# The two halves of each accumulator, added by a DMA with addition on GpSimd's queue in place of VectorE's addition

## What is computed

```
hidden = x
for i in (0, 1, 2):
    z   = einsum('bmd,bnd->bmnd', x, hidden).reshape(B, -1, D)
    cur = relu(einsum('bcd,co->bod', z, W[i]) + b[i])
    layers 0, 1: hidden, direct = cur[:, :100], cur[:, 100:]
    layer 2:     direct = cur
out = concatenate(direct of all layers).sum(-1)
```

## Time and profile before

| | before |
|---|---|
| median of 3 runs | 2800.74 us (2798.97 to 2800.89) |
| profiled execution, its own time | 2799.83 us |
| its span in the trace | 2798.1 us |
| granted clock of PE, mean | 0.997 of full speed |
| PE busy | 2707.5 us (97%) |
| DVE busy | 2722.4 us (97%) |
| ACT busy | 1763.7 us (63%) |
| POOL busy | 1.2 us, 11 instructions |

### The profile page before, as it was taken

How to read it: one execution, slowest core, us unless ns; L and a number is a source line. 1 busy time by engine, 2 the same in 40 slices (tenths; PEclk the granted TensorE clock), 3 DMA queues, 4 the chain that set the end, 5 groups by cost and what they waited for, 6 DMA issues and landing times.

```text
span 2798.1 us, 56046 instructions
## 1 busy us (share of the span) xinstructions
PE 2707.5 (97%) x18112; PEld 2642.5 (94%) x18112; DVE 2722.4 (97%) x3090; ACT 1763.7 (63%) x3178; POOL 1.2 (0%) x11
## 2 busy tenths in 40 slices
PE   1799999999999999999999999999999999999998
PEld 1799999999999999999999999999999999999998
DVE  3899999999999999999999999999999999999997
ACT  2566666666666666666666666666666666666664
POOL 0000000000000000000000000000000000000000
PEclk9999999999999999999999999999999999999999
DMA  8454544454454454454454454454454445444441
GB/s 193 110 126 109 129 123 108 118 134 108 123 129 109 112 138 110 117 131 112 109 138 114 113 130 117 108 132 120 108 128 121 111 122 129 109 117 124 119 112 54
DMA packets 346786, 333.97 MB, mean 119 GB/s; under 512 B 151970, under 2 KB 281614, under 8 KB 346638
## 3 DMA queue, kind: packets, MB, share of 16 engines
q1 hardware_dynamic: 346762, 333.67, 47.7%
HBM read 332.73 MB, written 8.37 MB: 122 GB/s over the span
## 4 chain that ended last, share of the span: by engine, by line
PE 93%; DMA 3%; DVE 1%; ACT 1%; SPq 1%; issue 1%; ACTq 0%; DVEq 0%
PE acc L620 63%; PE acc L621 28%; DMA xb<-x_by_unit 1%; PE summed L638 1%; PE turned L632 1%; DMA xb<-in_L_rec_b_dram 1%; ACT z_high L495 0%; DMA w_rows_again<-in_L_rec_W_dram 0%; DVE z_low L354 0%; DMA xb<-in_L_rec_W_dram 0%; DVE w_split L327 0%; ACT w_split L523 0%; ACT hid L514 0%; DVE z L350 0%; SPq L170 0%
## 5 line engine op out<-in xcount | busy, mean ns | idle before, releaser
L620 PE MATMUL acc<-w_split,z_high 128*128 128x400 f32 (+1 forms) x8832 | 2656.2, 368 | 71.8 <-DVE z_low L354 64.7
L621 PE MATMUL acc<-w_split,z_low 128*128 128x200 f32 (+1 forms) x8832 | 2252.9, 255 | 0.0
L620 PEld LDWEIGHTS acc<-w_split,z_high 128*128 128x128 f32 (+1 forms) x8832 | 1662.2, 188 | 119.8 <-issue 86.2
L495 ACT ACTIVATE z_high<-z 128x1024 fp32r<-128x1024 f32 (+2 forms) x1152 | 1181.9, 1026 | 898.1 <-DVE z L350 812.6
L621 PEld LDWEIGHTS acc<-w_split,z_low 128*128 128x128 f32 (+1 forms) x8832 | 1691.4, 192 | 0.0
L354 DVE TENSOR_TENSOR z_low<-z,z_high 128x1024 fp32r<-128x1024 f32 (+2 forms) x1152 | 1373.2, 1192 | 7.7 <-ACT z_high L495 7.0
L350 DVE TENSOR_TENSOR z<-hid,xb 128x1024 f32<-128x1024 f32 (+1 forms) x1024 | 1232.2, 1203 | 8.4 <-ACT hid L514 5.4
L514 ACT ACTIVATE hid<-turned 32x128 f32<-32x128 f32 x768 | 205.3, 267 | 8.9
L511 ACT ACTIVATE hid<-turned 96x512 f32<-96x512 f32 x256 | 150.1, 586 | 35.1 <-PE turned L632 33.3
L361 DVE TENSOR_TENSOR s<-acc,half 128x200 f32<-128x200 f32 x384 | 144.6, 377 | 9.8 <-ACT half L500 9.8
L339 DVE TENSOR_TENSOR z<-x_left,x_right 118x896 f32<-118x896 f32 x128 | 140.2, 1096 | 0.0
(11 more groups left out here) (21 smaller groups left out, 35.9 us busy)
## 6 DMA issues: line engine op xcount, KB each, us to landing
xb<-x_by_unit SPq DMA_DIRECT2D x384, 384.0 KB, 4.3
x_right<-x_by_unit SPq DMA_DIRECT2D x384, 136.5 KB
xb<-x_by_unit SPq DMA_DIRECT2D x384, 128.0 KB, 4.9
xb<-x_by_unit SPq DMA_DIRECT2D x128, 336.0 KB
xb<-x_by_unit SPq DMA_DIRECT2D x128, 84.0 KB
x_left<-x_by_unit SPq DMA_DIRECT2D x384, 19.5 KB
xb<-in_L_rec_W_dram SPq DMA_DIRECT2D x6, 600.0 KB, 8.6
x_by_unit<-in_r_x_dram SPq DMA_DIRECT2D x128, 19.5 KB
```

What stands on the lines that cost most here:

```text
L495: nc.scalar.activation(z_high[slot][0:rows, 0:n * T], z[slot][0:rows, 0:n * T], ACT.Copy).then_inc(high, 1)
L620: nc.tensor.matmul(a[:, 0:2 * O], z_high[slot][0:rows, tok], w, start=(c == 0), stop=False, skip_group_check=True)
L621: last = nc.tensor.matmul(a[:, 0:O], z_low[slot][0:rows, tok], w[:, 0:O], start=False, stop=(c == chunks - 1), skip_group_check=True)
```

## The change

The addition leaves DVE. ACT copies both halves of `acc[l]` to SBUF in one instruction (400 columns in place of 200), the first half to where `s[l]` lies and the second beside it, in one tensor `both[l]`. GpSimd then issues a DMA that adds the second to the first in place (`fold`), and its landing raises `s_in[l]` by 16. PE may write the accumulator anew as soon as ACT's copy is done.

```diff
-        s = {0: sb("s0", [P, 2, P]), 1: sb("s1", [P, 2, P]), 2: sb("s2", [P, 2, HID])}
-        half = {l: sb(f"half{l}", [P, 2, HID]) for l in range(3)}
+        both = {0: sb("both0", [P, 2, 2, P]), 1: sb("both1", [P, 2, 2, P]), 2: sb("both2", [P, 2, 2, HID])}
+        s = {l: both[l][:, 0, :, :] for l in range(3)}
...
+            def fold(l, u):
+                pool.wait_ge(half_in[l], u + 1)
+                pool.dma_start(s[l][:, :, 0:HID], both[l][:, 1, :, 0:HID], accum_op=ALU.add).then_inc(s_in[l], 16)
+
+            def period(n, layer0=True):
+                fold(1, n)
+                if layer0:
+                    fold(0, n + 2)
+                fold(2, n - 1)
...
-            def sums(l, u):
-                dve.wait_ge(half_in[l], u + 1)
-                if not (isinstance(u, int) and u == 0):
-                    dve.wait_ge(direct_in[l], u)
-                nc.vector.tensor_tensor(s[l][:, :, 0:HID], acc[l][:, 0:O].rearrange("p (h o) -> p h o", o=HID), half[l][:, :, :], ALU.add)\
-                  .then_inc(s_in[l], 1)
-
             def directs(l, rows, q):
...
-                dve.wait_ge(s_in[l], u + 1)
+                dve.wait_ge(s_in[l], 16 * (u + 1))
...
-                sums(1, n)
...
-                if layer0:
-                    sums(0, n + 2)
...
-            def second_half(l, u, last):
+            def halves(l, u, last):
 
                 act.wait_ge(freed, RING + last + 1)
-                nc.scalar.activation(half[l][:, :, :], acc[l][:, O:2 * O].rearrange("p (h o) -> p h o", o=HID), ACT.Copy)\
+                if not (isinstance(u, int) and u == 0):
+                    act.wait_ge(direct_in[l], u)
+                nc.scalar.activation(both[l][:, :, :, 0:HID], acc[l][:, 0:2 * O].rearrange("p (k h o) -> p k h o", k=2, o=HID), ACT.Copy)\
                   .then_inc(half_in[l], 1)
 
             def dup(l, u):
-                act.wait_ge(s_in[l], u + 1)
+                act.wait_ge(s_in[l], 16 * (u + 1))
...
             def acc_free(l, u):
-                pe.wait_ge(s_in[l], u)
+                pe.wait_ge(half_in[l], u)
```

More of the change, by code:

```diff
@@ L317, in _ @@
                                     base=STEPS - 1, pattern=[[STEPS, BT]], channel_multiplier=-1).then_inc(consts, 1)
+            def fold(l, u):
[6 more added lines that the diff above has]
+                fold(2, n - 1)
+            fold(0, 0)
+            fold(0, 1)
+            fold(1, 0)
+            fold(0, 2)
+            for n in range(1, UNITS):
+                period(n, layer0=n + 2 < UNITS)
+            fold(2, UNITS - 1)
         @block.vector
@@ L400, in _ @@
                     lows(1, 1, L0_ROWS, L0_CHUNKS)
-                    sums(0, 0)
                 if k == 2:
                     directs(0, 0, 0)
-                if k == 3:
-                    sums(0, 1)
             dve.wait_ge(w_low_done, 1 + 2 * GROUPS)
@@ L418, in _ @@
             lows(at + 4, slot_of(at + 4), L0_ROWS, L0_CHUNKS)
-            sums(1, 0)
-            sums(0, 2)
             directs(1, 0, 0)
@@ L441, in period @@
                 lows(base + 2, slot(2), P, group_chunks(2))
-                if before2:
-                    sums(2, n - 2)
                 q = 4
@@ L479, in _ @@
             product12(2, UNITS - 1, 1, 0, at, slot_of(at))
-            sums(2, UNITS - 2)
             for g in range(1, GROUPS):
@@ L485, in _ @@
             lows(at + 3, slot_of(at + 3), P, group_chunks(3))
-            sums(2, UNITS - 1)
             directs(2, last, 3)
@@ L533, in _ @@
                     highs(1, 1, L0_ROWS, L0_CHUNKS)
-                    second_half(0, 0, 0)
+                    halves(0, 0, 0)
                     act.wait_ge(consts, 4)
@@ L538, in _ @@
                     hidden(0, 0, 0)
-                    second_half(0, 1, 1)
+                    halves(0, 1, 1)
                 if k == 5:
@@ L548, in _ @@
             highs(at + GROUPS, slot_of(at + GROUPS), L0_ROWS, L0_CHUNKS)
-            second_half(1, 0, at + 3)
-            second_half(0, 2, at + 4)
+            halves(1, 0, at + 3)
+            halves(0, 2, at + 4)
             dup(1, 0)
@@ L566, in period @@
                 if before2:
-                    second_half(2, n - 2, base - 1)
+                    halves(2, n - 2, base - 1)
                 if j == 0:
@@ L580, in period @@
                 highs(base + q + 1, slot(q + 1), P, group_chunks(1))
-                second_half(1, n, base + 3)
+                halves(1, n, base + 3)
                 highs(base + q + 2, slot(q + 2), P, group_chunks(2))
                 if layer0:
-                    second_half(0, n + 2, base + 4)
+                    halves(0, n + 2, base + 4)
                 if before2 and j == 1:
@@ L601, in _ @@
             hidden(1, UNITS - 1, 1)
-            second_half(2, UNITS - 2, at - 1)
+            halves(2, UNITS - 2, at - 1)
             for g in range(GROUPS):
@@ L605, in _ @@
             results(1, last)
-            second_half(2, UNITS - 1, at + 3)
+            halves(2, UNITS - 1, at + 3)
             results(2, last)
```

## The result

| | before | changed |
|---|---|---|
| median | 2800.81 us (2798.97 to 2801.43, 4 runs) | 3326.22 us (3309.96 to 3335.73, 4 runs) |
| ratio | | 1.187, 95% interval 1.182 to 1.192 |
| span of the profiled execution | 2798.1 us | 3322.3 us |
| mean granted clock of PE | 0.997 | 0.942 |

The changed kernel is slower by 525 us, or 18.7%. The prediction had the sign and the place of the loss, but 52 us in place of 525, and the time lies far above its range.

A forecast was written before the change was run, and what follows sets the result against it. DVE was taken as the bound by a hair over PE. A middle period of 20.23 + 4.9 - 3.75 = 21.38 us adds 39 us over 125 periods, the ends 13 us: 2852 us, 1.8% slower, range 2768 to 2990 us.

The forecast's parts named there:

- What bounds the kernel: In the long middle DVE fills its 21.07 us period without slack; PE follows at about 20.76 us.
- The price of the additions: Three additions per period leave DVE, 0.28 us each, 0.84 us together, so DVE's work falls to 20.23 us.
- ACT's wider copy: ACT's copy of 400 columns takes 0.51 us, adding 0.5 us per period, hidden as ACT is 63% busy.
- The window of 3.75 us: DVE waits at `directs(1)` only if L, from ACT's copy end to the landing DVE sees, is over 3.75 us.
- The formula 20.23 + (L - 3.75): DVE's period in us: its work without additions plus what L, copy's end to landing, exceeds the window by.
- L = 4.9 us: Time from the end of ACT's copy to the landing DVE sees, taken from a 128 KB `xb` load's landing.
- The upper bound of 6.8 us: Bound from above on L, copy's end to landing: the longest landing of an `xb` load.
- I cost that at nothing too: The added DMA bytes, about 0.3 MB per period beside 2 MB of `xb` loads, were claimed to cost nothing.
- Rival 1: The sum lands inside its window, L under 4.3 us, and PE is the bound: 2779 us, 0.8% faster; chance 0.37.
- the draw: L between 4.3 and 4.6 us: the wait at `directs(1)` eats the additions' gain; 2794 to 2806 us; chance 0.07.
- Rival 3: Making GpSimd's DMA pieces waits for DVE instructions, L grows up to 1.13 us to 6.0 us: 2996 us; chance 0.08.
- `dup` on ACT: `dup(1)` stood 4.0 us after the copy's end; it follows DVE's wait for the sum and does not lead it.

The follow-up runs named there:

- The best kernel: Changed kernel with later readers of layer 1 and 0 sums and layer 0's store issued after the token loads: 2773.6 us, ratio 0.991.
- experiment 4: Changed kernel with the readers of the sums of layers 1 and 0 put two to three groups later: 2801.3 us, ratio 1.0008.
- experiment 2: Changed kernel with each xb load from unit 2 on bringing one chunk in place of up to eight: 2798.9 us.
- experiment 1: Changed kernel with GpSimd's DMAs copying the second half over the first instead of adding it: 3019.5 us.
- experiment 6: Changed kernel with layers 1 and 0 laid out as 128 pieces of 800 bytes per DMA in place of 256 of 400: 3250.7 us.
- experiment 5: Changed kernel with layer 0's store issued after the token loads: 3246.9 us; also with late readers: 2773.6 us; both moves with additions on DVE: 2794.8 us.
- experiment 9: Changed kernel with 24 small matmuls on PE ahead of layer 2's last group; sums not right, only time read: 3276.5 us.
- experiment 3: Changed kernel with only layer 2's sum by DMA, layers 1 and 0 added by DVE as before: 2785.8 us, ratio 0.9956.
- experiment 7: Changed kernel with plain copies in place of the additions, issued from ACT's queue instead of GpSimd's: 3228.6 us.
- experiment 8: Changed kernel with only layer 1's sum by DMA, the other two added on DVE: 3376.4 us.

## Why the prediction was wrong

**What bounds the kernel: right.** DVE full at 21.07 us, PE close behind at 20.76 us. The best kernel, in which PE alone is the bound, ran at 20.82 us per period.

**The price of the additions, 0.84 us for three: right.** In experiment 4, in the three periods of four in which DVE stood for at most 0.05 us, its period was 20.28 us, where the prediction had 20.23 us. What the time could gain was less, as foreseen, because PE follows: 0.16 us a period for layer 2 alone, 0.25 us for all three with late readers and the moved store.

**ACT's wider copy, 0.51 us and hidden: right** (0.51 us at 1508.86, and 0.498 us on average for L502).

**The window of 3.75 us: right.** The formula 20.23 + (L - 3.75) gives 23.4 us for the L of 6.9 measured above, and 44 periods at full clock lasted 23.9 us on average. Experiment 4 removed the loss by moving the readers alone, with landings as long as before.

**L = 4.9 us: this is the step that failed.** The term "I take 4.9 us, the landing of the 128 KB load" was measured as 6.9 us in the period shown and 10.1 us in a fourth one (copy's end at 1556.31, sum at 1566.37); over the periods from 300 to 2600 us the median was 7.3 us, and 9.2 us in the fourth ones. Two things were taken wrongly. The landing of an `xb` load counts from its issue, while L also has the 0.3 us from ACT to GpSimd. And the adding DMA is another kind of transfer: with thin loads its L is already 3.9 us (experiment 2), and beside the loads it is held up more than an `xb` load is, 7.0 us from issue to landing against 5.0 us for the 128 KB load in the same kernel. Why it is held up more stays open in part. A plain copy in few packets landed in 5.0 us (experiment 1), but making the pieces twice as large changed layer 1's landing by only 0.2 us (experiment 6), so their size of 400 bytes is not the reason. Two windows of the DMA list show the hold-up, from the issue at 1509.66 to about the first of its packets, and from there to the landing:

```profile
q1 hardware_dynamic: 201, 0.68, 101.3%
```

```profile
q1 hardware_dynamic: 368, 0.67, 72.3%
q0 software_dynamic: 458, 0.17, 41.0%
```

From 1509.6 to 1512.4 us only the loads' queue has packets, at 101% of all engines. The sum's queue has its first one at 1512.68, 3.0 us after the issue, where it took 1.8 us with thin loads, and needs until 1516.2. (The 458 packets of the second window are those of layer 1's sum and of a part of layer 0's.) I had seen the engines' share of 1.00, called it a reason for a larger value, and then let a favourable reason cancel it. The upper bound of 6.8 us was no bound: it was a landing of another kind of transfer, and L reached 11.3 us.

The Trainium skill's price (DMA: Bandwidth & Descriptors, Anatomy of one DMA — SWDGE (gpsimd) path), about 2.0 us fixed plus bytes at 436 GB/s, an estimate of 2.2 us here, comes near where nothing else runs: 2.5 to 2.8 us from issue to landing for layer 2's adding DMA, 1.9 us for the shortest plain copy. Beside the loads the measurement was 6.6 us for the DMA shown, 4.4 us more than the estimate.

**"I cost that at nothing too" for the traffic beside the loads: wrong in size as well.** The cover over the `xb` loads held, and no wait on `xb` became long. But a fourth period that was a little late before was made worse by the long waits (the store ahead of the loads: 79 us by experiment 5), and PE ran at half clock after many of its pauses (50 us came back in experiment 9). Neither was a term of the sum. With 23.9 us in place of 21.07 for the bulk of the 125 periods, 350 us, and these two, 129 us, and 18 us at the ends and in the setup (13 were predicted), some 500 of the 525 us are named; the two single effects were measured one at a time and may overlap with the rest. The mean says how much is the latency: with the mean L of 7.5 us over all periods the formula gives 24.0 us, 2.9 us over before, and the periods lasted 25.2 us. The prediction's own path, with the right L, thus carries some 360 of the 525 us. Of the other 1.2 us a period, 0.6 us are DVE's waits for ACT's high parts (77 us from 200 to 3200 us), and ACT in turn waited for PE's freed slots (202 us in the same stretch). What the rest is stays open.

**Rival 1 and the draw** are out for the kernel as it was changed. Their mechanism was right where its condition holds: with thin loads (landing 3.5 us) the time was 2799 us, where the draw had 2794 to 2806, and for layer 2 alone 2786 us. **Rival 3**, GpSimd against DVE, is refuted as a cause: DVE's products beside GpSimd's issues still start 1.0 to 1.13 us apart as before, layer 2's first packets all came 1.41 to 1.44 us after the issue while DVE was 97% busy (experiment 3), and with no issue on GpSimd at all layer 1's landing was still 6.8 us (experiment 7).

**`dup` on ACT** waits to the same moment as DVE (1516.25 in both), as foreseen, and does not lead.

## What to carry to other kernels

Price a DMA on a path by a transfer of the same kind (adding or plain, from the same queue), beside the same traffic at the same moment; if there is none, take the wait for full engines as an addition and not as a tie-break. What a transfer costs is its latency less the window to its first reader, so before giving it up, look whether you can move the readers: here the same DMAs went from 18.7% slower to 0.9% faster by moving nine calls (eight readers and one store). Where a few DMAs sit in a quiet stretch, they can be taken alone, as layer 2's were, at a fraction of the work.

## Unexpected behaviour of the hardware in these runs

- The plain copies went in 48 packets per DMA from GpSimd's queue, on average in 229 from ACT's; with addition GpSimd's queue also used 229 (18,432 and 88,064 for 384 DMAs). By layer the adding DMAs used 272 packets for 256 pieces of 400 bytes (34,816 for 128 DMAs in experiment 8) and 144 for 128 pieces of 800 bytes (18,432 in experiment 3).
- GpSimd's issue of an adding DMA took 1.18 to 1.20 us for 256 pieces and 0.84 to 0.89 us for 128 pieces, the latter also beside a DVE that was 97% busy (experiment 3).
- The first packet of an adding DMA of 256 pieces came 3.0 us after the start of its issue beside the full loads and 1.8 us beside the thin ones; that of 128 pieces with idle engines after 1.4 us, and of the plain copy of 128 pieces after 1.1 us.
- After a pause of 3.6 us PE ran 3.4 us at half clock, beginning 1.4 us after it had resumed.
